# Linear attention stage of a graph-transformer kernel: projections of q and k ahead of the values, one square in place of two, scans moved

## What is computed

```python
def _feature_map(x, w):
    xs = x * SCALE
    proj = jnp.einsum('bhnc,hcm->bhnm', xs, w)
    sq = 0.5 * jnp.sum(xs * xs, axis=-1, keepdims=True)
    return jnp.exp(proj - sq) / np.sqrt(M)
...
k_sum = jnp.sum(k, axis=2)
D = jnp.einsum('bhnm,bhm->bhn', q, k_sum)[..., None] + EPSILON
ktv = jnp.einsum('bhnm,bhnc->bhmc', k, v)
out = jnp.einsum('bhnm,bhmc->bhnc', q, ktv) / D
```

## Time and profile before

| | us |
|---|---|
| median of three runs | 3685.99 |
| the profiled execution's own time | 3677.07 |
| its span | 3674.9 |
| its mean granted TensorE clock | 0.901 |
| first run of the stage (layer 1), first to last matmul | 121.9 to 599.2 |
| second run (layer 2), first to last matmul | 2507.3 to 2947.0 |

### The profile page before, as it was taken

One profiled execution on the slowest core, in us unless ns is written; L12 is line 12 of the kernel. 1 busy time (PEld: TensorE's weight loads), 2 busy tenths in 40 slices (PEclk: granted clock), 3 DMA queues, 4 the chain that ended last, 5 costly groups with the idle time before them and its releaser, 6 DMA issues. The chain is left out here.

```text
span 3674.9 us, 50549 instructions
## 1 busy us (share of the span) xinstructions
PE 3017.5 (82%) x18054; PEld 2566.6 (70%) x18054; DVE 2341.4 (64%) x3813; ACT 1533.2 (42%) x2623; POOL 456.0 (12%) x301
## 2 busy tenths in 40 slices
PE   7799998877998997887795699786999966886695
PEld 4699987745887996776793233375999944776694
DVE  7544453836832546995766678665755757996775
ACT  6555573212112333552233577322544502553245
POOL 0688850200000000000004200000000000000000
PEclk8799998988999998998897799888899877997897
DMA  6332214784215444215212221353110085214211
GB/s 203 56 44 31 22 13 125 219 192 106 73 39 128 150 133 124 62 50 145 50 33 69 56 48 36 113 161 84 47 32 23 22 186 156 57 43 121 53 45 44
DMA packets 253098, 311.68 MB, mean 85 GB/s; under 512 B 98738, under 2 KB 182423, under 8 KB 252265
## 3 DMA queue, kind: packets, MB, share of 16 engines
q1 hardware_dynamic: 178109, 276.77, 28.0%
q0 software_dynamic: 74784, 32.32, 5.0%
HBM read 227.47 MB, written 80.57 MB: 84 GB/s over the span
## 5 line engine op out<-in xcount | busy, mean ns | idle before, releaser
L438 POOL DMA_INDIRECT adj_d<-key_val,key_off x160 | 337.8, 2111 | 173.6 <-issue 149.5
L3038 DVE TENSOR_TENSOR expert_wgel<-expert_gel,expert_wps 128x417 f32<-128x417 f32 (+1 forms) x384 | 202.7, 584 | 67.9 <-PE expert_wps L2963 60.8
L2026 PE MATMUL gat10att_ops<-gat10att_h,gat10att_p 125*125 x1600 | 195.3, 279 | 48.1 <-DVE gat10att_p L2002 48.1
L2026 PE MATMUL gat00att_ops<-gat00att_h,gat00att_p 125*125 x1600 | 197.2, 279 | 45.4 <-DVE gat00att_p L2002 45.3
L2026 PEld LDWEIGHTS gat10att_ops<-gat10att_h,gat10att_p 125*125 125x125 f32 x1600 | 183.8, 192 | 59.9 <-issue 59.9
L2026 PEld LDWEIGHTS gat00att_ops<-gat00att_h,gat00att_p 125*125 125x125 f32 x1600 | 182.9, 189 | 59.8 <-issue 59.8
L3010 ACT ACTIVATE expert_gel<-expert_hps 128x417 f32<-128x417 f32 (+1 forms) x384 | 194.1, 519 | 56.1 <-DVE expert_wgel L3038 48.0
L1329 PE MATMUL fc_ops<-fc_w_hi,fc_x_lo 128*125 128x384 f32 x480 | 164.3, 342 | 17.0 <-DVE fc_w_lo L1377 17.0
L596 PE MATMUL perf_wide<-y_lo,perf_qk_hi 128*128 128x416 f32 (+1 forms) x432 | 156.0, 361 | 26.4 <-DVE perf_v L802 10.1
L1185 PE MATMUL fc_ps<-y_lo,fc_w_hi 128*128 128x512 f32 (+1 forms) x432 | 154.5, 358 | 20.5 <-DVE fc_w_lo L1227 20.5
L1329 PE MATMUL fc_ops<-fc_w_lo,fc_x_hi 128*125 128x384 f32 x480 | 163.8, 341 | 0.0
(11 more groups left out here) (484 smaller groups left out, 8142.3 us busy)
## 6 DMA issues: line engine op xcount, KB each, us to landing
fc_w<-in_L_mix_fc_w SPq DMA_DIRECT2D x96, 384.0 KB
adj_d<-edge_zero SPq DMA_DIRECT2D x4, 2734.4 KB
gat00proj_adj<-adj_d POOLq DMA_DIRECT2D x20, 546.9 KB, 6.9
gat00att_sh<-shift_d SPq DMA_DIRECT2D x16, 546.9 KB
gat10att_sh<-shift_d SPq DMA_DIRECT2D x16, 546.9 KB
perf_w<-in_L_mix_qkv_w SPq DMA_DIRECT2D x18, 384.0 KB
perf_w<-in_L_mix_W_qkv SPq DMA_DIRECT2D x18, 384.0 KB
attn_d<-perf_o SPq DMA_DIRECT2D x12, 560.0 KB
```

Source lines behind the costliest of these rows:

```text
L438: nc.gpsimd.indirect_dma_start(out=adj_flat[u], out_offset=bass.IndirectOffsetOnAxis(ap=key_off[:, c:c + 1], axis=0), in_=key_val[:, c:c + ...
L2026: ins = pe.matmul(ops[0:TP, u, b, t * w:(t + 1) * w], p[:, s, (t0 + t) * TP:(t0 + t + 1) * TP], h[:, s, bass.ds(hd, 1), :], start=(s == 0 ...
L3038: dve.tensor_tensor(wgel[:, q % W, 0:cn], gel[:, q % 3, 0:cn], wps[:, q % 3, 0:cn], ALU.mult).then_inc(wgel_done, 1)
```

## The change

- The weights of q and k are loaded and split first, then features and biases, then the weights of the values. `project` comes ahead of `values` at the start and between pairs; it no longer waits for the values' copies, but for the exponentials that read its banks; `values` uses the banks in the order of `phi_banks` and waits, from tile 4 on, for the rests of q's blocks; the pairs with u = 0 begin with a wait for all five copies of the values.
- With 384 features, the first three of the ten tiles of `outputs(1)` come ahead of the projections.
- ScalarE squares first, rows 0 to 127 in one instruction in place of two of 32 rows, and then writes the high parts, now across partitions; the rests are made in the partitions in which they are computed. A new semaphore `hi_done` says that the high parts are there.
- Two scan tiles, not four, come ahead of `keep_ktv(0)`, the other eight in one piece behind it. Heads 3 and 6 are scanned between `rests` and `keep_values` of the pairs with u = 1, head 0 between `rests(0)` and `keep_values(0)`, head 7 in the first pair of the last iteration; nothing is scanned in the last pair or behind it.

```diff
+    early = 3 if mb_n == 3 else 0
...
-                load_v(0)
-                sp.wait_ge(w_split, 1)
                 load_qk(0)
                 load_features(0)
...
+                sp.wait_ge(w_split, 1)
+                load_v(0)
                 sp.wait_ge(w_split, 2)
                 load_qk(1)
...
+                def values(i, split):
...
                     for t in range(NT):
+                        if t >= 4 and t % 2 == 0:
+                            pe.wait_ge(lo_done, g * 6 + 3 + t // 2 - 1)
...
-                            elif u == 0:
-                                pe.wait_ge(v_done, i * 5 + c + 1)
+                            elif not (isinstance(g, int) and g == 0):
+                                j = max(j for j in range(units) if phi_banks[j % ring] == c)
+                                pe.wait_ge(exp_done, g * units - units + j + 2)
...
+                    if u == 0:
+                        pe.wait_ge(v_done, i * 5 + 5)
...
                     q_features(1)
+                    if early:
+                        outputs(1, 0, early)
                     if not last:
-                        pe.wait_ge(exp_done, g * units + units + 1)
+                        project(g + 1, i * 3 + 3 + 2 * u)
                         if u == 1:
-                            values(i + 1)
-                        project(g + 1, i + u, 1 - u)
-                    outputs(1)
+                            values(i + 1, i * 3 + 4)
+                    outputs(1, early, NT)
...
-                values(0)
-                project(0, 0, 0)
+                project(0, 1)
+                values(0, 2)
...
+                            act.wait_ge(s_done, g * 6 + n + 1)
+                            act.wait_ge(add_done, g * 6 + n + 1)
+                            act.activation(sq[:, n % 2, 0:cn], wide[:, c, 0:cn], ACT.Square, bias=bias(1, 0, 128), scale=root)
+                            for r0 in (0, 64):
+                                ins = act.activation(more[r0:r0 + 32, 0:cn], wide[r0 + 32:r0 + 64, c, 0:cn], ACT.Square,
+                                                     bias=bias(1, r0 + 32, r0 + 64), scale=root)
+                            ins.then_inc(sq_done, 1)
                             for x in range(2):
                                 r0 = 64 * x
-                                act.activation(ab[r0:r0 + 64, side, x, :, c0:c0 + cn],
-                                               wide[r0:r0 + 64, c, 0:cn].unsqueeze(1).to_broadcast([64, 2, cn]),
-                                               ACT.Identity, bias=bias(0, r0, r0 + 64))
+                                ins = act.activation(ab[64 - r0:128 - r0, side, x, :, c0:c0 + cn],
+                                                     wide[r0:r0 + 64, c, 0:cn].unsqueeze(1).to_broadcast([64, 2, cn]),
+                                                     ACT.Identity, bias=bias(0, r0, r0 + 64))
+                            ins.then_inc(hi_done, 1)
...
+                            dve.wait_ge(hi_done, g * 6 + n + 1)
...
+                    hd = i * 3 + 1 + u if scan is not None and not last else None
...
-                        scan.start(dve, g + 1, 0, g + 1)
-                        scan.tiles(dve, g + 1, 0, 0, 4)
+                        scan.start(dve, hd, 0, hd)
+                        scan.tiles(dve, hd, 0, 0, 2)
                     keep_ktv(0)
                     if u == 0 and not (isinstance(i, int) and i == HP // 2 - 1):
                         split_w(v_parts, i * 3 + 3)
-                    if scan is not None:
-                        scan.tiles(dve, g + 1, 0, 4, 6)
+                    if hd is not None:
+                        scan.tiles(dve, hd, 0, 2, NT)
+                        scan.finish(dve, hd, 0)
                     keep_out(0)
-                    if scan is not None:
-                        scan.tiles(dve, g + 1, 0, 6, NT)
-                        scan.finish(dve, g + 1, 0)
                     keep_ktv(1)
...
+                        rests(g + 1)
                         if u == 1:
+                            if scan is not None:
+                                scan.head(dve, i * 3 + 3, 0, i * 3 + 3)
                             keep_values(i + 1)
-                        rests(g + 1)
                     keep_out(1)
...
-                split_w(v_parts, 0)
-                split_w(qk_parts, 1)
+                split_w(qk_parts, 0)
                 split_features(0)
...
+                split_w(v_parts, 1)
+                rests(0)
                 if scan is not None:
                     dve.wait_ge(scan.mask_ld, 32)
                     scan.head(dve, 0, 0, 0)
                 keep_values(0)
-                rests(0)
...
-                if scan is not None:
-                    scan.head(dve, HP + 1, 0, HP + 1)
```

More of the change, by code:

```diff
@@ L572, in _ @@
                     pe.nop().then_inc(s, 1)
-                def values(i):
-                    pe.wait_ge(w_split, i * 3 + 1)
+                def values(i, split):
+                    g = i * 2
+                    pe.wait_ge(w_split, split)
+                    if not isinstance(i, int):
+                        pe.wait_ge(exp_done, g * units + 1)
                     for t in range(NT):
+                        if t >= 4 and t % 2 == 0:
+                            pe.wait_ge(lo_done, g * 6 + 3 + t // 2 - 1)
                         for kb in range(KB):
                             for n, (yp, wp) in enumerate(passes):
-                                ins = pe.matmul(wide[0:TP, t // 2, t % 2 * 256:t % 2 * 256 + 256],
+                                ins = pe.matmul(wide[0:TP, phi_banks[t // 2], t % 2 * 256:t % 2 * 256 + 256],
                                                 y_parts[yp][:, kb, t * TP:(t + 1) * TP], v_parts[wp][:, :, kb, :],
@@ L583, in values, with project @@
                             ins.then_inc(v_proj, 1)
-                def project(g, i, u):
-                    pe.wait_ge(w_split, i * 3 + 2 + u)
+                def project(g, split):
+                    pe.wait_ge(w_split, split)
                     for side in range(2):
@@ L647, in k_t_v, with outputs @@
                         ins.then_inc(ktv_done, 1)
-                    def outputs(x):
-                        pe.wait_ge(ktv_kept, g * 2 + x + 2)
-                        pe.wait_ge(o_kept, g * 4 + 2 * x + 1)
+                    def outputs(x, first, end):
+                        if first == 0:
+                            pe.wait_ge(ktv_kept, g * 2 + x + 2)
+                            pe.wait_ge(o_kept, g * 4 + 2 * x + 1)
                         for bank, t0, tn in o_tiles:
-                            for t in range(t0, t0 + tn):
+                            for t in range(max(t0, first), min(t0 + tn, end)):
                                 if t in (0, 3, 6):
@@ L659, in outputs @@
                                                     start=(mb == 0), stop=(mb == mb_n - 1))
-                        ins.then_inc(o_done, 1)
+                        if end == NT:
+                            ins.then_inc(o_done, 1)
                     if per_head:
                         pe.wait_ge(feat_split, g + 1)
+                    if u == 0:
+                        pe.wait_ge(v_done, i * 5 + 5)
                     pe.wait_ge(s_done, g * 6 + 5)
@@ L815, in rests @@
                                               ALU.add).then_inc(add_done, 1)
+                            dve.wait_ge(hi_done, g * 6 + n + 1)
                             for x in range(2):
                                 rows, other = slice(64 * x, 64 * x + 64), slice(64 - 64 * x, 128 - 64 * x)
-                                high = ab[rows, side, x, 0, at].bitcast(F32)
+                                high = ab[other, side, x, 0, at].bitcast(F32)
                                 if biased:
                                     ins = dve.scalar_tensor_tensor(
-                                        out=ab[other, side, x, 0, at], in0=wide[rows, c, 0:cn],
+                                        out=ab[rows, side, x, 0, at], in0=wide[rows, c, 0:cn],
                                         scalar=bpair[rows, 0, 1 - side:2 - side], in1=high,
@@ L824, in rests @@
                                 else:
-                                    ins = dve.tensor_tensor(ab[other, side, x, 0, at], wide[rows, c, 0:cn], high, ALU.subtract)
+                                    ins = dve.tensor_tensor(ab[rows, side, x, 0, at], wide[rows, c, 0:cn], high, ALU.subtract)
                             ins.then_inc(lo_done, 1)
```

29 lines of the change are left out of this document (10 added, 19 removed).

## The result

The changed kernel took 3589.47 us (median of 3 runs, 3585.98 to 3595.45) against 3685.99: a ratio of 0.9745, 95% interval 0.9714 to 0.9776. The forecast was 3582, the range 3560 to 3622. Ten more runs of it, among the experiments, gave 3580.36 to 3595.34 with a median of 3588.2, and the kernel before had a median of 3681.8 beside them (3679.1 to 3683.2 beside the three groups of experiments).

What follows compares the result with a forecast made beforehand. TensorE was taken as the bound, with waits and low clocks to remove. Savings of 25.2 + 55.4 + 4.5 + 14.0 = 99.1 took the profiled 3677.1 to 3578.0; as runs lie above the profiled one, forecast 3582, range 3560 to 3622.

Steps and rivals of the forecast that it cites:

- Second run, the 361.6 us: Second run behind its start: kept sum in time, all six middles 17.9 us, transitions shorter; 55.4 us saved.
- a wait of under 3 us costs 12.6: Slow middles of pairs, second run: a 2.69 us wait for the kept sum costs 12.6, nearly 10 through the clock.
- First run: TensorE's waits in the first run fall from 32.7 to 7.5 us; 25.2 us saved.
- A block: Blocks of q or k: 128-row square taken as 0.51 us; VectorE sets the pace at 3.85 in the second run.
- rival C: The 128-row square costs 1.02 us, first rests come later, ScalarE paces the first run again: about 10, 3592; chance 0.07.
- ScalarE 15% less busy on squares: One of the signs that would show the forecast right: ScalarE's busy time on squares falls by 15%.
- Start of the second run: Up to the end of pair 0's features: waits of 6 and 5.4 us remain, 4.5 us saved.
- End: Stage's end: last outputs take 4.5 us, not 7.5, and SyncE's 11.0 us wait goes; 14.0 saved together.
- Rival A: Second run: the kept sum stays late in pairs 1 and 3, price 2 x 12, 3606 us; chance 0.16.
- Rival B: Middles of pairs 1 to 4: the clock falls anyway, only idle time is saved; 36 us, 3618; chance 0.08.
- Rival D: Slower: heads 0, 3 and 6 hold up VectorE and TensorE if a scan row is missing; 3690 us; chance 0.02.
- Rival E: The start goes better, with the values' weights ahead of the mask: 3574 us; chance 0.07.

Runs made afterwards that it cites:

- the two squares: The changed kernel with the 128-row square taken apart into the two 32-row squares it replaced: 3608.0 us (0.9792).
- the run with head 7 last: The changed kernel with the scan of head 7 back behind everything on VectorE: 3595.76 us (0.9768).
- the run with three tiles: The changed kernel with three scan tiles instead of two ahead of the copy of the kept sum: 3595.28 us (0.9754).
- three tiles moved: The changed kernel with the last three tiles of heads 0, 3 and 6 behind the copies of the values: 3583.59 us (0.9749).
- the run with four tiles: The changed kernel with four scan tiles instead of two ahead of the copy of the kept sum: 3613.91 us (0.9804).

## Why the prediction was right

**Second run, the 361.6 us: right, 52.5 of 55.4.** The step "a wait of under 3 us costs 12.6" is shown in both directions: taking two tiles away in the old kernel gives all six middles back, putting two back in the new one loses pairs 1 and 3. The middles saved 46.5 (12.5 + 10.5 + 11.0 + 12.4, and 0.1 in pair 5), as forecast. The transitions saved 6.0 instead of 8.9: those with values are 55.6 and 54.2, not 53.2. Their wait was sized 1.5 (TensorE's 46.5 us in that sum are 46.7 by its own terms, 20.8 + 21.5 + 4.4, so 1.2) and was 2.2 and 1.8, and the features behind it begin slowly (clock 0.94 in the window 2629.70:2685.30). And one of the two waits, at pair 2's start, is not VectorE's alone: one of about 2 us stays there when VectorE is early (2.17 and 1.91 in two of the runs).

**First run: right in the sum, 25.8 of 25.2, and there with some luck.** Idle time was to fall to 7.5 and fell to 11.3 (451.5 - 440.2): the features' waits are 7.4, not 6.6; the 1.0 in q's projections and the 1.9 at the loop's turn were not forecast at all. In exchange busy time, which I had held fixed, fell from 444.6 to 440.2. Part of that fall is the execution's: the old order had 444.6 and 443.2 in its two profiles, the changed kernel's first run 439.6 to 443.8 in eight. Part is the long waits at the start, which went: around them the granted clock was 0.50 from 173.2 to 181.4 us. The step "It is the bound, and only its waits can go" put the clock at nothing, and failed: the rows under the two squares show 0.50 to 0.66 for 5 us behind waits of 2.6 to 3.9 us in the first run as well. Tested alone were the order at the start, the squares and the early outputs; what `values` behind `project` gives between the pairs of the first run was not.

**A block: right.** 520 ns for the square, 0.51 taken; rival C, 1.02, is out. But its worth to the kernel was sized too low: "the last rests come some 2.3 us earlier" gives 7 us, and undoing it cost 12.9 in the first run, 7.2 of them idle time, where a repeat can be off by 3 or 4. The sign "ScalarE 15% less busy on squares" is loosely put: the squares' own time fell by 24% in the second run (73.5 to 55.5 us), all of ScalarE's work on the blocks by 13% (135.6 to 117.5).

**Start of the second run: right, 4.6 of 4.5.** The waits were forecast as 6 and 5.4 and are 6.5 and 6.6. **End: right,** 3.0 and 11.0, of which the run with head 7 last gives back 7 to 11.

**Rival A** did not come. The sum stands ready 0.44 us ahead in pair 1, where I had 0.7. Its price of 12 is not a constant: the run with three tiles had a wait of 1.0 us in both pairs for 1.2 each. The row that I argued from, 0.72 at the last outputs behind a wait of 1 us, is real too; both outcomes follow one wait.

**Rival B** did not come either: the same 65-column matmuls through the same banks run at 1.00 in all six middles, also in the old kernel with two tiles moved. The Trainium skill ("TensorE: Matmul & The Clock Gate", "A second HAM failure mode: psum-queue depth-cycling") tells of such cycling through banks, in a kernel of bf16 matmuls of 512 columns, as what makes the clock fall and rise. By that rule it should have kept falling here; no run here shows that, and the measurement decides: in the profile of after the clock is low at the first matmuls of both runs and behind waits of 1.8 us and more, and nowhere else in the stage.

**Rival D** did not come: no tile waited for a row in the changed kernel. But the row's load is real, and three tiles moved were enough to meet it. **Rival E** did not come: q's projections waited 6.5.

**The forecast of 3582** lies 7 us under the median of the three runs and 6 under that of the ten, and the measured time is inside its range. The stretches of the stage account for 2.2 of them (96.9 instead of 99.1). The rest is not pinned to a step: it is of the size by which executions of one kernel differ, and the base of the sum was one profiled execution, with its first matmul at 121.9 us, earlier than in any other profile here.

## What to carry to other kernels

A buffer that was late by 1.0 us cost 1.2 here and one late by 2.7 us cost up to 12.6, so look in the windows for equal work at two clocks, and ask by how much each wait must shrink, not only what it sums to. Before work is moved into an engine's idle time, ask what load its end sets off: the next row's load started with the last tile, and the idle time that it needed was not free. Cut two profiles at the same places before comparing spans, since here a stage that nobody touched moved by 18 us. And profile the same kernel again before a few us of busy time are put down to an edit: here the clock fell behind one wait in one execution and not in the next, worth up to 4 us in a stretch.

## What the runs showed that I had not expected

Behind waits for a kept sum, ahead of 65-column matmuls: after 0.99 us the 40 matmuls took 4.55, after 1.87 us 7.59, after 2.70 us 8.40 and 6.84, and in the kernel before, after 2.21 to 2.69 us, 7.31 to 8.66. After 1.01 us they took 4.58 in one kernel and 6.5 in another. Once low, the clock stayed low although TensorE did not stand still: these windows follow the wait of pair 1 in the run with four tiles, at 1.2 GHz for 20 us and at 2.4 GHz again in the projections.

```profile
2620.46:2625.00 4.54, 4.54 (x23) 4.54 (x24) 4.35 (x7) 0.00 (x0) 0.00 (x0) 0.53 0.02 4
...
2636.00:2641.50 5.50, 5.50 (x20) 5.31 (x20) 0.29 (x1) 2.93 (x5) 0.00 (x0) 0.53 0.01 1
2641.50:2646.00 4.50, 4.50 (x26) 4.44 (x25) 0.00 (x0) 1.64 (x4) 0.00 (x0) 1.00 0.00 0
```

Ahead of the wider feature matmuls of the first run the same wait had both outcomes, in two executions of the same program. These are the first 5 us behind the wait at pair 5's start, 2.26 us in the changed kernel's profile and 2.27 us in that of its repeat:

```profile
548.65:553.65 5.00, 5.00 (x25) 4.36 (x26) 3.22 (x9) 4.88 (x12) 0.00 (x0) 1.00 0.13 33
```

```profile
553.30:558.30 5.00, 4.98 (x19) 4.97 (x20) 3.24 (x9) 4.31 (x10) 0.00 (x0) 0.67 0.13 32
```

So at 2.3 us neither the length of the wait nor the program decides, and at 1.0 us its length does not; what does stays open and was not tried. The seven waits of 1.87 to 2.70 us ahead of 65-column matmuls that these profiles hold were all followed by the low clock.

TensorE loses 1.7 to 2.3 us at the turn of the program's loop, with no releaser: in the first run of the changed kernel and its variants, and in the second run where VectorE is early. That it is the loop's turn is read from its place, since pair 4, which is written out behind the loop, has no such wait. It was not tried.
